# Context of tiles 5 to 14 as four 64x64 products on the quarters of the matmul array

## What is computed

```python
q = (h @ Wq.T).reshape(b, s, 8, 64).transpose(0, 2, 1, 3)
k = (h @ Wk.T).reshape(b, s, 1, 64).transpose(0, 2, 1, 3)
v = (h @ Wv.T).reshape(b, s, 1, 64).transpose(0, 2, 1, 3)
q, k = apply_rope(q, pos_ids), apply_rope(k, pos_ids)
scores = jnp.einsum('bkgsd,bktd->bkgst', qg, k) / jnp.sqrt(64.0)
attn = jax.nn.softmax(scores, axis=-1)
ctx = jnp.einsum('bkgst,bktd->bkgsd', attn, v)
x = res + ctx.reshape(b, s, 512) @ Wo.T
# then ada_rms, silu(h @ Wg.T) * (h @ Wu.T) @ Wd.T, and the second layer (16 heads of 32)
```

## Time and profile before

| | |
|---|---|
| Median of 3 runs | 915.97 us (915.91 to 916.86) |
| Profiled execution, its own time | 916.34 us |
| Span of its trace | 914.4 us |
| PE, PEld busy | 875.1, 735.3 us |
| DVE, ACT, POOL busy | 571.9, 471.8, 412.4 us |
| Granted clock, mean over the span | 0.994 of full speed |

### The profile page before, as it was taken

How to read it: one execution, slowest core, us unless ns; L and a number is a source line. 1 busy time by engine, 2 the same in 40 slices (tenths; PEclk the granted TensorE clock), 3 DMA queues, 4 the chain that set the end, 5 groups by cost and what they waited for, 6 DMA issues and landing times.

```text
span 914.4 us, 16039 instructions
## 1 busy us (share of the span) xinstructions
PE 875.1 (96%) x6168; PEld 735.3 (80%) x6168; DVE 571.9 (63%) x943; ACT 471.8 (52%) x861; POOL 412.4 (45%) x315
## 2 busy tenths in 40 slices
PE   4888999999999999999999999999999999998997
PEld 3777888888888888887887888888888888877785
DVE  5666465565556556557556676585675775766776
ACT  5465454454444544545537556455455464453662
POOL 2355554454544554546347544453444443421331
PEclk9899999999999999999999999999999999999999
DMA  9810322122222221112132122121121221200001
GB/s 336 315 33 29 115 74 89 70 77 85 70 81 81 70 81 70 70 70 87 70 115 70 71 70 82 69 82 58 59 93 58 81 82 70 71 1 13 25 24 36
DMA packets 30971, 73.19 MB, mean 80 GB/s; under 512 B 4272, under 2 KB 4784, under 8 KB 30896
## 3 DMA queue, kind: packets, MB, share of 16 engines
q1 hardware_dynamic: 30032, 72.07, 22.7%
q10 hardware_dynamic: 864, 0.10, 0.1%
HBM read 67.96 MB, written 4.19 MB: 79 GB/s over the span
## 4 chain that ended last, share of the span: by engine, by line
PE 84%; DVE 5%; issue 5%; POOL 3%; ACT 2%; DMA 1%; SPq 0%; POOLq 0%; ACTq 0%; DVEq 0%
PE ps L462 25%; PE ps L464 24%; PE ps L463 24%; PE ps L550 2%; PE ps L718 1%; PE ps L706 1%; PE ps L532 1%; PE ps L517 1%; PE ps L696 1%; POOL qr L332 1%; PE ps L649 1%; DVE al L1001 1%; PE ps L674 1%; PE ps L579 1%; POOL hl L325 1%
## 5 line engine op out<-in xcount | busy, mean ns | idle before, releaser
L344 POOL TENSOR_TENSOR gul<-rgu,guh 128x1024 fp32r<-128x1024 f32 x64 | 156.6, 2446 | 187.6 <-ACT guh L1378 187.6
L1006 DVE TENSOR_TENSOR xres<-ps,xres 128x512 f32<-128x512 f32 x256 | 174.5, 687 | 88.8 <-PE ps L464 88.7
L462 PE MATMUL ps<-h2h,guh 128*128 128x512 f32 x512 | 205.9, 402 | 0.6 <-issue 0.6
L464 PE MATMUL ps<-h2l,guh 128*128 128x512 f32 x512 | 199.8, 390 | 0.0
L463 PE MATMUL ps<-h2h,gul 128*128 128x512 f32 x512 | 199.5, 390 | 0.0
L464 PEld LDWEIGHTS ps<-h2l,guh 128*128 128x128 f32 x512 | 96.1, 188 | 20.9
L462 PEld LDWEIGHTS ps<-h2h,guh 128*128 128x128 f32 x512 | 96.2, 188 | 20.4 <-issue 1.1
L463 PEld LDWEIGHTS ps<-h2h,gul 128*128 128x128 f32 x512 | 96.3, 188 | 18.8
L462 PE MATMUL ps<-wdh,ah 128*128 128x512 f32 x256 | 101.0, 395 | 5.5 <-DVE al L1001 3.0
L1400 ACT CAST ah<-af 128x512 fp32r<-128x512 f32 x64 | 39.7, 620 | 119.2 <-DVE af L1019 110.5
L464 PE MATMUL ps<-wdl,ah 128*128 128x512 f32 x256 | 100.1, 391 | 0.0
(11 more groups left out here) (165 smaller groups left out, 1672.1 us busy)
## 6 DMA issues: line engine op xcount, KB each, us to landing
rgu<-gu SPq DMA_DIRECT2D x64, 512.0 KB, 3.6
rwd<-WdT SPq DMA_DIRECT2D x64, 256.0 KB, 2.7
xt<-xT SPq DMA_DIRECT2D x16, 256.0 KB, 3.5
out<-xres SPq DMA_DIRECT2D x15, 256.0 KB, 2.8
xres<-x SPq DMA_DIRECT2D x1, 2560.0 KB, 11.9
adaw<-adaT SPq DMA_DIRECT2D x1, 2048.0 KB, 15.9
wst<-WqkvT SPq DMA_DIRECT2D x4, 320.0 KB, 5.9
adaw<-ln_twT SPq DMA_DIRECT2D x4, 256.0 KB, 4.0
```

What stands on the lines that cost most here:

```text
L344: pool.tensor_tensor(gul[i][:, :], rgu[i][:, :], guh[i][:, :], ALU.subtract).then_inc(m_gul, 1)
L462: pe.matmul(dst, lh, rh, start=start, stop=False)
L464: return pe.matmul(dst, lh, rl, start=False, stop=stop)
L1006: dve.tensor_tensor(at, bank(BD[i % 2]), at, ALU.add).then_inc(m_x, 1)
```

## The change

For tiles 5 to 14 (`quarters`) the context is computed without the zero blocks: four products of 64x64 weights by 256 columns, one for each sequence b and head parity i. Product (b, i) reads partitions 64i to 64i+63 and writes bank XB[2 + i], partitions 64(i xor b) onwards; so each lies on a quarter of the array of its own. PE has one wait more, for a_x, since XB[3] is now written here. ch and cl are made by four instructions of 64 partitions by 256 elements each, in the place of one of 128 by 512; of each four, those with b = 1 read the other half of the partitions than they write. The signal comes with the last of the four.

```diff
+        def quarters(t):
+
+            return HEAD < t < NT - 1
...
-                for b in range(2):
-                    mm = pe.matmul(ps[:, ctx_bank(t), 256 * b:256 * (b + 1)], bdv[t % 2][:, b, :],
-                                   pT[:, :, S * b:S * (b + 1)], start=True, stop=True)
+                if quarters(t):
+                    pe.wait_ge(a_x, t)
+                    for b in range(2):
+                        for i in range(2):
+                            r, c = slice(HD0 * i, HD0 * (i + 1)), HD0 * (i ^ b)
+                            mm = pe.matmul(ps[c:c + HD0, XB[2 + i], 256 * b:256 * (b + 1)], bdv[t % 2][r, b, r],
+                                           pT[r, :, S * b:S * (b + 1)], start=True, stop=True)
+                else:
+                    for b in range(2):
+                        mm = pe.matmul(ps[:, ctx_bank(t), 256 * b:256 * (b + 1)], bdv[t % 2][:, b, :],
+                                       pT[:, :, S * b:S * (b + 1)], start=True, stop=True)
...
-                dve.tensor_tensor(by_entry(cl[:, :, :]), bank(ctx_bank(t)).rearrange("p (b j s) -> p j b s", b=2, j=KT),
-                                  by_entry(ch[:, :, :]), ALU.subtract).then_inc(a_cl, 1)
+                if quarters(t):
+                    for i in range(2):
+                        for b in range(2):
+                            r, c = slice(HD0 * i, HD0 * (i + 1)), HD0 * (i ^ b)
+                            ins = dve.tensor_tensor(cl[r, :, S * b:S * (b + 1)],
+                                                    ps[c:c + HD0, XB[2 + i], 256 * b:256 * (b + 1)]
+                                                    .rearrange("p (j s) -> p j s", j=KT),
+                                                    ch[r, :, S * b:S * (b + 1)], ALU.subtract)
...
-                act.copy(by_entry(ch[:, :, :]), bank(ctx_bank(t)).rearrange("p (b j s) -> p j b s", b=2, j=KT)
-                         ).then_inc(a_ch, 1)
+                if quarters(t):
+                    for i in range(2):
+                        for b in range(2):
+                            r, c = slice(HD0 * i, HD0 * (i + 1)), HD0 * (i ^ b)
+                            ins = act.copy(ch[r, :, S * b:S * (b + 1)],
+                                           ps[c:c + HD0, XB[2 + i], 256 * b:256 * (b + 1)]
+                                           .rearrange("p (j s) -> p j s", j=KT))
```

More of the change, by code:

```diff
@@ L990, in low_ctx @@
                 wait(dve, a_wo, t)
-                dve.tensor_tensor(by_entry(cl[:, :, :]), bank(ctx_bank(t)).rearrange("p (b j s) -> p j b s", b=2, j=KT),
-                                  by_entry(ch[:, :, :]), ALU.subtract).then_inc(a_cl, 1)
+                if quarters(t):
[6 more added lines that the diff above has]
+                                                    ch[r, :, S * b:S * (b + 1)], ALU.subtract)
+                else:
+                    ins = dve.tensor_tensor(by_entry(cl[:, :, :]),
+                                            bank(ctx_bank(t)).rearrange("p (b j s) -> p j b s", b=2, j=KT),
+                                            by_entry(ch[:, :, :]), ALU.subtract)
+                ins.then_inc(a_cl, 1)
             def add_x(t):
@@ L1346, in high_ctx @@
                 wait(act, a_wo, t)
-                act.copy(by_entry(ch[:, :, :]), bank(ctx_bank(t)).rearrange("p (b j s) -> p j b s", b=2, j=KT)
-                         ).then_inc(a_ch, 1)
+                if quarters(t):
[5 more added lines that the diff above has]
+                                           .rearrange("p (j s) -> p j s", j=KT))
+                else:
+                    ins = act.copy(by_entry(ch[:, :, :]),
+                                   bank(ctx_bank(t)).rearrange("p (b j s) -> p j b s", b=2, j=KT))
+                ins.then_inc(a_ch, 1)
             def square2(t):
```

## The result

| | before | after |
|---|---|---|
| Median | 916.08 us (6 runs) | 921.38 us (6 runs) |
| Ratio to before, 95% interval | | 1.0053 [1.0043, 1.0063] |
| Profiled execution, span | 916.34, 914.4 | 918.88, 917.0 |

What follows compares the result with a forecast made beforehand. PE is busy 875.1 of 914.4 us, but in eight of ten steps al ends last, by very little. 3.5 (eight steps) + 0.8 (after tile 14) - 0.1 = +4.2 us on 915.97 gives 920.2 us; range 916.3 to 922.4.

Steps and rivals of the forecast that it cites:

- The way of the loss: Steps with a prep: longer ch and cl delay af, guh, gul, wdl, stat, xn, exp, al and PE, by 0.44 us each.
- The quarters on PE: Context on PE: four products run side by side, 0.78 us against 0.86, saving about 0.08 us a tile.
- The wait for a_x: PE's new wait for the residual add of the tile before, at the context: costs nothing, the add being long past.
- ch and cl: Copies on ACT and DVE: four each, ch taking 1.53 us, cl 1.75; af 0.92 us later.
- rival A: DVE overlaps although the halves change: cl takes 0.34 us an instruction, +1.1 us in all, 917.1 us; chance 0.13.
- 0.44 a step: Eight steps with a prep: wdl, stat, xn, al and PE each come 0.44 us later, 3.5 us in all.
- gul's length: POOL's gul behind the context: still takes 2.40 us, running from 185.62 to 188.02.
- Step 10: Step without a prep, after tile 9: PE keeps its saving of 0.08 us, so about 0.1 us shorter.
- Step 14: Behind tile 14's context: wqh stands behind the longer ch, so wqh and PE come 0.8 us later.
- B: Not slower: af moves by less than 0.35 us, PE keeps 0.4 to 0.8 us in all, 915.3 us; chance 0.13.
- C: Changing the form on PE costs nothing: ch starts 0.14 us earlier still, +2.6 us in all, 918.6 us; chance 0.05.
- D: Quarters of 256 columns run one by one on PE: 1.2 us more a tile, near 930 us; chance 0.03.

Runs made afterwards that it cites:

- PE's part alone: Changed kernel with ch and cl each made by one instruction again, context still in quarters: 914.35 against 915.94 us for the kernel before, ratio 0.9984.
- halves swapped: Changed kernel with the second sequence's scores sent to the other bank, ch and cl one instruction each: 914.85 against 916.19 us before, ratio 0.9985.
- the straight copies: Kernel before with ch and cl made by four instructions each, every one reading the partition half it writes: 920.69 against 915.94 us, ratio 1.0050.
- the copies alone: Kernel before, context in one bank, with ch and cl made by the change's four instructions each: 923.14 against 915.94 us, ratio 1.0074.
- the stat early: Changed kernel with POOL's stat for the next prep ahead of the four MLP pieces behind the context: 913.42 against 915.94 us before, ratio 0.9974.

## Why the prediction was right

**The way of the loss** was the forecast's: copies, af, guh, gul, wdl, stat, xn, exp, al, PE. Moving the stat cut it, and the loss was gone but for step 14; taking the copies out removed all of it; taking PE's part away and leaving the copies made the loss greater.

**The quarters on PE**: forecast 0.78 for the block and 0.08 saved. From L522 to the third MLP matmul 1.36, where before there were 1.44:

```profile
178.36 0.27 PE L518 MATMUL ps<-idn,qr 128*128 128x128 f32 x1
...
179.80 0.39 PE L464 MATMUL ps<-h2l,guh 128*128 128x512 f32 x1
```

So 0.08 are saved there, as forecast. But less of it is left at the end of the group. The matmuls behind the block follow each other some 0.23 to 0.24 apart for a while (180.13 to 180.37) before they are back at the 0.226 to 0.227 of a steady stream. In the kernels with quarters 0.02 of the saving is left behind fifteen of them in half of the steps, and 0.05 to 0.09 in the others, and the same tile differs from one kernel to the next. The change of form is not needed for such spacing: before the change the first matmuls behind the context stood 0.23 apart too, and in the changed kernel it comes back from 186.04 on, where a weight load waits 0.09 for al. What decides how long it lasts I can't say; it was not tried apart. The wait for a_x cost nothing: the first pass comes 0.20 behind L522, the 0.11 of before and the 0.09 that I had put for the form.

**ch and cl**: forecast 1.53 and 1.75, measured 1.50 and 1.76 (181.00 to xt's start at 182.76). The choice of ACT's row for DVE, where the trace of before had none, was the one that decided between the forecast and rival A, and it was the right one for the right reason, the changing halves: where they don't change, DVE's starts are 0.34 apart. Counted from L522, af is 0.94 later (forecast 0.92).

**0.44 a step** was too small: 0.55. The term that failed is gul's length. al of the group behind the context comes into hl, as I wrote, and ends at 186.04, 0.24 after gul's start: gul takes 2.49 and not 2.40. I had this overlap cost only PE, inside its other wait; it costs the chain 0.09, the rest being small. The other traces bear it out: in the same place gul takes 2.40 where al has ended before it starts (PE's part alone, halves swapped), 2.40 where al ends 0.11 after its start (the straight copies), and 2.49 again with the copies alone, where al ends 0.23 after it.

**Step 10** was to gain 0.08 and gained nothing: the quarters keep 0.02 there, and al, late by now behind the context, takes that back. **Step 14** brought 1.27: 0.49 up to its context, as in the other steps with a prep, and 0.78 behind it, forecast 0.8. In step 14 of the changed kernel, against the earlier trace rows:

```profile
421.31 1.50 ACT L1374 CAST ch<-ps 64x256 fp32r<-64x256 f32 x4
...
422.83 1.91 ACT L1444 CAST wqh<-w1st 128x2048 fp32r<-128x2048 f32 x1
...
424.82 4.59 POOL L392 TENSOR_TENSOR wql<-w1st,wqh 128x2048 fp32r<-128x2048 f32 x1 [3.58 <-ACT wqh L1444]
...
425.98 3.98 DVE L1024 TENSOR_TENSOR al<-af,ah 128x512 fp32r<-128x512 f32 x1
```

wqh starts behind the last of four casts, wql behind wqh, and al ends behind wql. The sum of the terms was 3.5 + 0.8 - 0.1 = 4.2; the steps show 4.3 + 0.8 and nothing gained, 5.1, and the medians 5.3. (The forecast's 0.6 a step gives 921.5 by its own sum, not the 921.6 written there.)

**The rivals.** A (DVE overlaps) falls by the starts 0.43 to 0.44 apart. B (the chain has the slack) falls by wdl without idle time; af would have had to move by less than 0.35 and moved by 0.94. Its price was sound all the same: where the copies are one instruction each, the steps show 0.68 less, within the 0.4 to 0.8 us that it named. C (no price for the form) falls by the 0.34 behind the block, D by the two rounds of four.

## What to carry to other kernels

Where an engine that is 96% busy waits 0.04 us for another's result, look behind that result: here the slack of the whole chain was 0.43 us. And a saving on the engine that seems to be the bound pays only if its followers don't grow. Dividing an evacuation by partition halves costs more than the count: each instruction that reads or writes other partitions than the one before also loses its overlap with it (0.38 and 0.44 from start to start, where 0.27 and 0.34 were possible). Better to change the layout upstream, where it is free, so that the result comes out whole; and to move a short step (0.55 us) out from behind two long ones of a filler, which here gave more than the change itself could.

## What the runs showed of the hardware that I had not expected

- ACT too loses its overlap (starts 0.27 apart become 0.38 for casts of 0.37) when the half of the partitions that is read, or the half that is written, changes between two instructions.
- Two row halves of the array may write one bank at once if they write other partitions: the block is as long as with two banks (0.59 from its first pass to the next matmul's start).
- In these traces the exp's table load waits for none of the exp's operands: with the stat early it ran at 187.99, at once behind xn, when the subtraction that makes the exp's input had not begun (188.38).
- Beside one POOL instruction of 4.6 us a DVE subtraction of 0.69 takes 3.3 us; beside four of a quarter it takes 1.2.
